# Attention with tails in a ring of steps: the tails' work put behind other work on TensorE, VectorE, ScalarE and GpSimd

## The reference, cut to what matters

```python
x = x + attn0(layernorm(x))      # x is (4, 512, 128); causal softmax attention, 16 heads of 8
x = x + moe(layernorm(x))        # 8 experts, top 2 of softmax(x @ Wr), a capacity per expert
x = x + layer1_attention(x)      # gated linear recurrence, 16 heads of 64, layer norms and an FFN inside
x = x + layer1_ffn(x)

# moe: which tokens an expert keeps
topv, topi = top_k(softmax(xt @ Wr), 2); topv = topv / sum(topv)
onehot = one_hot(topi, 8); rank = cumsum(onehot, axis=0)
keep = (rank <= capacity) * onehot
```

## Time and profile before

| | us |
|---|---|
| median of 3 runs | 694.78 (694.71 to 694.92) |
| profiled execution, its own time | 693.35 |
| span of the profiled execution | 691.6 |
| PE busy | 573.8 (83%) |
| DVE busy | 422.8 (61%) |
| ACT busy | 301.4 (44%) |
| POOL busy | 166.2 (24%) |

### The profile page before, as it was taken

The page is one execution under the profiler, slowest core; times in us unless marked ns, Lnnn a source line. Parts: engine busy times, 40 slices in busy tenths (PEclk is TensorE's granted clock), DMA queues, the critical chain, the costliest instruction groups (busy, mean ns, idle before and its releaser), DMA issues.

```text
span 691.6 us, 9159 instructions
## 1 busy us (share of the span) xinstructions
PE 573.8 (83%) x3296; PEld 429.7 (62%) x3296; DVE 422.8 (61%) x1040; ACT 301.4 (44%) x435; POOL 166.2 (24%) x180
## 2 busy tenths in 40 slices
PE   2488989998999851999980859889999999998997
PEld 1445556555556531687760638667887888787876
DVE  6676778878878623124223698698368936773241
ACT  3225554444555421255330634474347535662361
POOL 3001212252162254000005753361220013001100
PEclk9799999999999865899995899999999999999999
DMA  3314222123210031476401100010000000000000
GB/s 103 126 62 162 77 100 90 42 85 114 74 57 24 5 118 64 161 231 196 116 24 47 31 19 13 1 31 1 1 0 17 1 1 0 16 1 0 3 14 15
DMA packets 40909, 38.82 MB, mean 56 GB/s; under 512 B 3104, under 2 KB 31776, under 8 KB 40864
## 3 DMA queue, kind: packets, MB, share of 16 engines
q1 hardware_dynamic: 38816, 34.04, 15.7%
q0 software_dynamic: 2048, 4.20, 1.9%
HBM read 23.54 MB, written 14.68 MB: 55 GB/s over the span
## 4 chain that ended last, share of the span: by engine, by line
PE 60%; DVE 13%; issue 9%; POOL 7%; ACT 7%; DMA 3%; SPq 0%; DVEq 0%; POOLq 0%; ACTq 0%
PE ps L1830 6%; PE ps L1792 5%; PE ps L1566 5%; PE ps L1852 5%; PE ps L1537 4%; PE ps L1783 4%; PE ps L1933 4%; PE ps L1929 4%; PE ps L1853 4%; PE ps L1930 4%; PE ps L1856 3%; PE ps L1554 3%; DVE pm L966 3%; POOL xs_dram L497 2%; POOL PT L511 2%
## 5 line engine op out<-in xcount | busy, mean ns | idle before, releaser
L637 ACT ACTIVATE PT<-ps 128x768 f32<-128x768 f32 (+1 forms) x96 | 84.6, 883 | 80.7 <-PE ps L1554 79.4
L966 DVE TENSOR_REDUCE pm<-ps 128x4 f32<-128x512 f32 x160 | 104.5, 686 | 20.3 <-PE ps L1540 11.1
L511 POOL TENSOR_SCALAR_AFFINE_SELECT PT<-PT 128x512 f32<-128x512 f32 x64 | 39.9, 636 | 161.9 <-ACT PT L637 161.8
L1537 PE MATMUL ps<-KP,QS 128*128 128x512 f32 x160 | 67.6, 453 | 4.5 <-DVE pm L966 3.0
L1554 PE MATMUL ps<-QM,KP 128*128 128x512 f32 (+3 forms) x256 | 63.1, 350 | 0.4 <-DVE QM L980 0.4
L1566 PE MATMUL ps<-PT,V 128*32 128x128 f32 (+3 forms) x512 | 48.0, 471 | 14.1 <-POOL PT L511 14.1
L727 ACT ACTIVATE HT<-ps,cols 128x640 f32<-128x640 f32 x32 | 25.4, 794 | 57.1 <-PE ps L1783 57.1
L1537 PEld LDWEIGHTS ps<-KP,QS 128*128 128x128 f32 x160 | 29.5, 194 | 32.3 <-DVE pm L966 30.1
L1554 PEld LDWEIGHTS ps<-QM,KP 128*128 128x128 f32 x256 | 41.0, 197 | 10.3 <-issue 6.1
L1341 DVE TENSOR_TENSOR_SCAN zero<-decay,OG 128x512 f32<-128x512 f32 x32 | 42.2, 1320 | 1.1
L1792 PE MATMUL ps<-W,HT 128*128 128x128 f32 x320 | 37.9, 278 | 2.9 <-ACT HT L727 2.9
(11 more groups left out here) (284 smaller groups left out, 1305.5 us busy)
## 6 DMA issues: line engine op xcount, KB each, us to landing
qk_dram<-HL SPq DMA_DIRECT2D x8, 512.0 KB, 3.3
W<-in_eW SPq DMA_DIRECT2D x16, 256.0 KB, 3.5
QS<-qk_dram SPq DMA_DIRECT2D x64, 48.0 KB
KP<-qk_dram SPq DMA_DIRECT2D x64, 48.0 KB
xs_dram<-zero SPq DMA_DIRECT2D x4, 640.0 KB, 5.3
XS<-xs_dram SPq DMA_DIRECT2D x8, 320.0 KB, 4.8
ys_dram<-zero SPq DMA_DIRECT2D x8, 320.0 KB, 2.9
qk_dram<-HL SPq DMA_DIRECT2D x8, 256.0 KB, 3.4
```

What stands on the lines that cost most here:

```text
L511: g.affine_select(out=diag, in_=diag, pattern=[[0, 4], [1, P]], compare_op=ALU.is_ge, fill=0.0, base=0, channel_multiplier=-1).then_inc(se ...
L637: act.activation(PT[:, 2 * i:2 * i + 2, a:z], ps[:, 2 * (n % 2) + 2:2 * (n % 2) + 4, 0:z - a], ACT.Exp, scale=float(DK) ** -0.5).then_inc( ...
L966: v.tensor_reduce(pm[:, t, k, :], bank[n % 2].rearrange("p (i n) -> p i n", n=P), AXX, ALU.max).then_inc(pair_free[n % 2], 1)
L1537: mm = pe.matmul(to, QS[:, G % 2, t * P:(t + 1) * P], KP[:, G % 3, k, :, :].rearrange("p i n -> p (i n)"), start=True, stop=t != k)
```

## The change: what it does

- **TensorE.** The tail's product of g = 1, 2, 3 moves from in front of row scores 2 and 3 to behind them.
- **VectorE.** `add` and `ranks` move from behind row maximum 1 to behind row maximum 3. `stats_` moves from behind row maximum 3 to behind `minus_max`, in front of `add_max`. `norm` moves from in front of `add_max` to behind it. `place` moves from behind row maximum 3 to behind `add_max`. `make_halves` moves behind `minus_max`.
- **ScalarE.** `round_halves` moves from in front of exponential 3 to behind it.
- **Gate weights.** `gate_exp` and the five small operations on weights leave the tails; one exponential and five operations over all 16 tiles stand behind the last tail. `keep`, `dl`, `ex` and `w1t` grow for it.
- **GpSimd.** `rsqrt` moves behind `select(w, 1)`; the scatters of batches 0 and 1 are spread in pairs over the end of step g = 3 and the selects of the step behind it. In the last step their order is as it was.

```diff
@@ GpSimd, in the loop over w
+                late = before if w == NW - 1 else None
                 select(w, 0)
                 if at == 0 and before > 0:
-                    scatter(before - 1, range(7, 8))
+                    scatter(before - 1, range(2, 4))
+                if late is not None:
+                    scatter(late, range(0, 3))
+                select(w, 1)
                 if at == 1 and before >= 0:
                     rsqrt(varA, rsA, before + 1)
-                if at == 3 and before >= 0:
+                if at == 0 and before > 0:
+                    scatter(before - 1, range(4, 6))
+                if late is not None:
+                    scatter(late, range(3, 5))
+                select(w, 2)
+                if at == 0 and before > 0:
+                    scatter(before - 1, range(6, 8))
+                if at == 3 and before >= 0 and late is None:
                     if before == 0:
                         g.wait_ge(zeroed, 64)
-                    scatter(before, range(0, 3))
-                select(w, 1)
-                if at == 3 and before >= 0:
-                    scatter(before, range(3, 5))
-                select(w, 2)
+                    scatter(before, range(0, 2))
@@ ScalarE
-                if b and g == 3:
-                    gate_exp(b - 1)
...
                 exp_unit(w, 1)
                 exp_unit(w, 2)
+                exp_unit(w, 3)
                 if g == 0 and b + 1 < NB:
                     round_halves(b + 1)
-                exp_unit(w, 3)
@@ VectorE, in the loop over w
-                    row_max(w + 1, 0)
-                    row_max(w + 1, 1)
+                    for m in range(4):
+                        row_max(w + 1, m)
                 if b and g == 1:
                     add()
                 if b and g == 3:
                     ranks()
-                if rows_next:
-                    row_max(w + 1, 2)
-                    row_max(w + 1, 3)
-                if b and g == 1:
-                    stats_()
-                if b and g == 3:
-                    place()
...
                     for m in range(6, 10):
                         row_max(w + 1, m)
+                    minus_max(w + 1)
+                if b and g == 1:
+                    stats_()
                 if g == 0 and b + 1 < NB:
                     make_halves(b + 1)
-                if rows_next:
-                    minus_max(w + 1)
-                if b and g == 1:
-                    norm()
                 if b and g == 2:
                     take_logits()
                 if rows_next:
                     add_max(w + 1)
+                if b and g == 1:
+                    norm()
                 if b and g == 2:
                     choose()
+                if b and g == 3:
+                    place()
@@ TensorE, in the loop over w
                 key_scores(w, 0)
+                if rows_next:
+                    row_scores(w + 1, 2)
+                    row_scores(w + 1, 3)
                 if b and g == 1:
                     times_wo(b - 1)
                 if b and g == 2:
                     turn_normed(b - 1)
                 if b and g == 3:
                     ranks(b - 1)
-                if rows_next:
-                    row_scores(w + 1, 2)
-                    row_scores(w + 1, 3)
```

More of the change, by code:

```diff
@@ L194, in build @@
         posG = sb("posG", [P, 2 * NT], U32)
[L195 to L197 removed]
+        dl = sb("dl", [P, NT])
+        ex = sb("ex", [P, NT])
+        w1t = sb("w1t", [P, NT])
         wts = sb("wts", [P, 2 * NT])
@@ L655, in take_turn @@
                 act.activation(dst, tp_bank, ACT.Copy).then_inc(tp_free, 1)
-            def gate_exp(tb):
-                act.wait_ge(dl_done, tb + 1)
-                act.activation(ex[:, :], dl[:, :], ACT.Exp).then_inc(ex_done, 1)
             keep_x(0)
@@ L709, in _ @@
             take_last(1, 4, xn2T)
-            last_gate(0)
-            last_gate(1)
+            act.wait_ge(dl_last, 2)
+            act.activation(ex[:, :], dl[:, :], ACT.Exp).then_inc(ex_done, 1)
             act.activation(ready[:, :], mhalf[:, 0:1], ACT.Gelu)
@@ L1047, in place @@
                 def place():
+                    kb = keep[:, 2 * TB * b:2 * TB * (b + 1)]
                     v.wait_ge(tp_free, TURNS["ranks", b] + 1)
-                    v.tensor_reduce(keep[:, :], sel[:, :, :], AXX, ALU.add)
+                    v.tensor_reduce(kb, sel[:, :, :], AXX, ALU.add)
                     link(v.tensor_tensor(rank[:, :, :], rank[:, :, :], oh[:, :, :], ALU.mult))
@@ L1196, in place @@
                     v.wait_ge(last_free[h], 6)
-                    v.tensor_reduce(keep[:, n4], sel[:, n4, :], AXX, ALU.add)
+                    at = 2 * TB * b + 4 * h
+                    kb = keep[:, at:at + 4]
+                    v.tensor_reduce(kb, sel[:, n4, :], AXX, ALU.add)
                     step(v.tensor_tensor(rank[:, n4, :], rank[:, n4, :], oh[:, n4, :], ALU.mult))
                     step(v.tensor_reduce(pos[:, n4], rank[:, n4, :], AXX, ALU.add))
-                    at = 2 * TB * b + 4 * h
                     db = dump_row[:, at:at + 4]
                     step(v.tensor_tensor(pos2[:, n4], pos[:, n4], db, ALU.subtract))
-                    step(v.tensor_tensor(pos2[:, n4], pos2[:, n4], keep[:, n4], ALU.mult))
+                    step(v.tensor_tensor(pos2[:, n4], pos2[:, n4], kb, ALU.mult))
                     v.tensor_tensor(posS[:, b % 2, n4], pos2[:, n4], db, ALU.add).then_inc(pos_last, 1)
-                    v.tensor_tensor(posG[:, at:at + 4], pos[:, n4], keep[:, n4], ALU.mult)
-                def weigh():
-                    at = 2 * TB * b + 4 * h
-                    v.wait_ge(ex_last, h + 1)
-                    step(v.tensor_scalar(w1t[:, t2], ex[:, t2], 1.0, None, ALU.add))
-                    step(v.reciprocal(w1t[:, t2], w1t[:, t2]))
-                    wb = wts[:, at:at + 4].rearrange("p (t k) -> p t k", k=2)
-                    kb = keep[:, n4].rearrange("p (t k) -> p t k", k=2)
-                    v.tensor_tensor(wb[:, :, 0], w1t[:, t2], kb[:, :, 0], ALU.mult)
-                    step(v.tensor_tensor(w1t[:, t2], w1t[:, t2], ex[:, t2], ALU.mult))
-                    v.tensor_tensor(wb[:, :, 1], w1t[:, t2], kb[:, :, 1], ALU.mult)
-                return heads, add, norm, choose, place, weigh
+                    v.tensor_tensor(posG[:, at:at + 4], pos[:, n4], kb, ALU.mult)
+                return heads, add, norm, choose, place
             last_tail.done = 0
-            heads0, add0, norm0, choose0, place0, weigh0 = last_tail(0)
-            heads1, add1, norm1, choose1, place1, weigh1 = last_tail(1)
+            heads0, add0, norm0, choose0, place0 = last_tail(0)
+            heads1, add1, norm1, choose1, place1 = last_tail(1)
             heads0()
@@ L1232, in _ @@
             place1()
-            weigh0()
-            weigh1()
+            v.wait_ge(ex_done, 1)
+            gates = Order(lG, 0, 0)
+            gates(v.tensor_scalar(w1t[:, :], ex[:, :], 1.0, None, ALU.add))
+            gates(v.reciprocal(w1t[:, :], w1t[:, :]))
+            wb = wts[:, :].rearrange("p (t k) -> p t k", k=2)
+            kb = keep[:, :].rearrange("p (t k) -> p t k", k=2)
+            v.tensor_tensor(wb[:, :, 0], w1t[:, :], kb[:, :, 0], ALU.mult)
+            gates(v.tensor_tensor(w1t[:, :], w1t[:, :], ex[:, :], ALU.mult))
+            gates(v.tensor_tensor(wb[:, :, 1], w1t[:, :], kb[:, :, 1], ALU.mult))
             v.wait_ge(w1_in, 16 * 6)
```

32 lines of the change are left out of this document (8 added, 24 removed).

## The result

The changed kernel takes 712.98 us (median of 3 runs, 710.68 to 714.23) against 694.78: ratio 1.0258, 95% interval 1.0227 to 1.0289, slower by 18.2 us. Forecast were 708.0 in a range of 699.0 to 713.5: the side is right, the time 5.0 us more. Its profiled execution took 712.98, with a span of 711.2.

What follows compares the result with a forecast made beforehand. Bound: the PE and VectorE hand-over chain, where work before maximum 1 costs its whole length. Step terms +6.2, port +3.0 and clock +4.0 make +13.2 on 694.8: 708.0 us, range 699 to 713.5.

Steps and rivals of the forecast that it cites:

- Halves: Three g = 0 steps: exponential 3 goes first, so select and products finish earlier and QM starts sooner; -1.3 each, -3.9 us.
- Product, statistics: Three g = 1 steps: product costs 0.95 on PE's chain, statistics add 0.4 before QM; 12.55 against 12.77, -0.6 us in all.
- Normalisation: Three g = 2 steps: norm, waiting for POOL's power, delays maximum 0, and the transposes delay PE; +1.95 each, +5.9 us.
- Place: Steps 8 and 12: place takes 1.78 in front of maximum 0, having cost almost nothing where it stood; +3.6 us.
- Ranks: Steps 7 and 11: PE's 14 small matmuls go behind unit 3; -0.25 and +0.4, together +0.15 us.
- Weights: Five small VectorE operations leave places with slack and at the end stand under the wait for the rows; 0.
- Port: Five places between QM and maximum 0: VectorE operations lose part of a POOL select, 0.6 each; +3.0 us.
- Clock: Longer PE idles lower the granted clock in three of five steps (6, 8, 10, 12, 14), 1.33 each; +4.0 us.
- Last step: After step 14: place behind the normalisation delays POOL's first scatter to 241.3, then select 1 and products with V; +1.1 us.
- Cheap delay: Rival for the whole kernel: neither port nor clock costs anything; 701.0 us, chance 0.2.
- Dear delay: Rival: port and clock both at their high ends, perhaps the last step at low clock too; 713.8 us, chance 0.15.
- Slack takes it: Rival: the 1.21 us idle before maximum 4 absorbs a late first maximum; 695.0 us, no change, or 693.9; chance 0.08.

Runs made afterwards that it cites:

- the moved tiles: Kernel before with one unused tile of 192 bytes per partition behind wts, shifting all later tiles; nothing else differs: 700.39 us.
- the halves only: Kernel before with only make_halves moved behind minus_max and round_halves behind exponential 3: 691.71 us.
- the tiles at 256: Changed kernel with an unused 64-byte tile per partition behind wts, so later tiles lie 256 bytes further on than before, not 192: 713.22 us.
- the fill: Changed kernel plus the 64-byte tile, with four extra 512-column TensorE products behind key score 0 in steps 6, 8, 10, 12, 14: 707.68 us.
- the kernel with it divided and the scatters late: Kernel before with halves moved, weights computed once, place's last six operations behind minus_max, and GpSimd in the changed kernel's order: 691.06 us.
- the small selects: Changed kernel plus the 64-byte tile, with GpSimd's attention selects covering 8 columns of the diagonal block instead of 128: 700.30 us.
- the divided place: Kernel before with halves moved, weights computed once, and place's last six operations behind minus_max; GpSimd's order as before: 706.23 us.

## Why the prediction was right, and where it fell short

To compare terms, steps are taken at clock 1.00. Before: 187.9 us for steps 0 to 14 (step 0 at 13.02 from the moved tiles, steps 7 and 11 at 14.77 and 14.74 from the halves only, the rest as profiled; with the moved tiles step 11 took 15.11 at 1.00, so this is good to some 0.4). Changed: 194.0 (steps 7, 8, 11 and 12 at 13.61, 15.68, 13.61 and 14.01 from the tiles at 256, step 14 at 13.98 from the fill). That is +6.1, and the clock takes 6.3 in the changed kernel and 1.5 in before, +4.8.

- **Halves**, -3.9: measured -1.3, -1.3 and -1.8. Right; step 0 gave more, as allowed for. Step 2 is 0.3 longer, with the halves alone too (11.44 for 11.20); why isn't known.
- **Product, statistics**, -0.2 each: measured -0.35 each with the statistics moved. With the statistics left where they were, the product behind unit 3 doesn't delay maximum 4 (5.82 behind QM against 6.09); the 0.3 that those steps lost is the wait for `rstd`.
- **Normalisation**, +1.95 each and 0.6 of port, 2.55: measured 2.6 (13.89 against 11.31). Right in mechanism and size: of the 2.6, maximum 0 is 2.19 later (2.88 for 0.69), with 1.55 and 0.6 forecast.
- **Place**, +1.8 each and 0.6 of port, 2.4: measured 2.9 and 2.8 (15.68 against 12.77; 14.01 against 11.22). The port takes 0.83, since `place` meets both selects; the other 1.73 in front of maximum 0 is close to the 1.8 forecast.
- **Ranks**, +0.15 for both steps: measured -1.16 and -1.13. This step failed. It read from the earlier trace rows that unit 4 is there only at 136.45 and that `place` therefore cost nothing where it stood. But PE had come there late: from 133 to 135.8, with the products with V and a key score in front of that unit, it ran at a clock of 0.50 to 0.52 (the earlier trace rows has one microsecond of it). With the halves only, where it ran at 1.00, PE is done with units 4 and 5 at 135.21 and waits for `place` and the weights. The low clock had hidden a VectorE delay. Of the 1.16 the weights are 0.8, so **Weights**, 0, was wrong for the same reason; behind the rest is `place` (the kernel with it divided and the scatters late takes another 0.74 off step 7, 13.22 for 13.96). A line of the trace before could have warned: by its row the last weight operation ends at 136.73, and maximum 4 starts at 136.64, so there was no slack left even there.

```profile
136.56 0.17 DVE L1069 TENSOR_TENSOR wts<-w1t,keep 128x4 f32<-128x4 f32 x1
```

- **Port**, +3.0: by the rows of the small selects 3 x 0.55 + 2 x 0.83, 3.3. The Trainium skill ("SBUF — State Buffer", "Who interferes with whom") calls the port pair that VectorE and GpSimd share an exclusive lock. The two small operations agree, each held to a select's end; the row maxima, which read PSUM, ran beside selects at 0.65. For `norm` the high end of 1.22 was not reached.
- **Clock**, +4.0 for three of five steps: steps 8, 12 and 14 fell, by 1.1, 1.1 and 1.4. The number was luck in part. The same program with tiles 64 bytes on has the falls in steps 0, 6, 10 and 14 and none in 7, 8, 11 and 12. All in all the clock costs 4.8 more in these two traces.
- **Last step**, +1.1: measured +1.2 up to the first product on rows read back. The number is right, the path only in part. `posS` is there at 252.35 and the first scatter starts at 253.33, 8.52 behind the last QM where it was 8.04: +0.5 and not +1.1. Behind it TensorE ran at 0.50 from 258 on, where before parts of that stretch were at 1.00; that the other 0.7 comes from there isn't shown.

The parts together are 12.1 us for these stretches (+10.9 and +1.2), where the forecast had 13.2. The terms missed partly cancel, and that is luck: `ranks` (with the weights) was 2.4 too dear, while `place` and `norm` with their port, and the clock, were 2 too cheap. In the traces, what carried the result beyond 708 stood in no step of the prediction. Of the 4.9 us behind the last send, 3.2 are shown with nothing but the moved tiles, and adding 64 bytes took 4.6 away in the trace, though not in the median. The 1.8 ahead of the first QM isn't the change's: the kernels of the experiments have that QM at 42.91 to 44.95, the one with before's own order at 44.36, and one with all of the change's orders (the small selects) at 42.91.

Cheap delay (701.0) falls, as the port is shown by the small selects and the clock by the windows. Dear delay (713.8) gave about the measured time for the wrong reason. Slack takes it falls with the 2.15 of PE's idle in front of row scores 2. The scatters overran nothing here; and they had to be moved with `place`, as the divided place shows, where select 1 waited for them and steps 7 and 11 were 5 to 7 us longer. GpSimd's power behind select 1 was no term of the prediction: where `norm` isn't moved it costs the g = 1 steps 0.3 to 0.9.

## What to carry over

Where two engines hand a double buffer to and fro, work put in front of the first hand-over costs its whole length, work in the idle of the second half costs little; but look at what is queued behind each producer and each consumer on its own engine. Read slack only from a stretch at full clock: a slow TensorE makes VectorE's delays look free. A tile that grows moves all tiles behind it, so keep their distance when you compare, and look at products far from the edit.
